# A selective state-space block with attention and feed-forward on one core: ScalarE's next exponential moved ahead of second halves of its jobs, and two kinds of VectorE reads moved one scan later

## The reference

```python
x = x + mamba(keep_top_rows(x))        # rows by norm; 512 channels, 16 states, L = 1024
# inside mamba, per batch:
xi, z  = split(rmsnorm(x) @ in_proj)
xi     = silu(causal_conv4(xi) + conv_b)
dt,B,C = split(xi @ x_proj)
delta  = softplus(dt @ dt_w + dt_b)
for t: h = exp(delta*A)*h + (delta*xi)*B ;  y = sum_s h*C     # 16 states s per channel
y      = (y + xi*D) * silu(z) ;  return x + y @ out_proj
x = x + feed_forward(attention(x, cond, mask))
```

## Time and profile before

| what | value |
|---|---|
| three executions | 580.72, 580.25, 576.88 us |
| median | 580.25 us |
| the profiled execution, its time | 581.45 us |
| its span in the profile | 579.3 us |
| granted TensorE clock, mean over the span | 0.926 |

### The profile page before, as it was taken

The page is one execution under the profiler, slowest core; times in us unless marked ns, Lnnn a source line. Parts: engine busy times, 40 slices in busy tenths (PEclk is TensorE's granted clock), DMA queues, the critical chain, the costliest instruction groups (busy, mean ns, idle before and its releaser), DMA issues.

```text
span 579.3 us, 7844 instructions
## 1 busy us (share of the span) xinstructions
PE 481.0 (83%) x2753; PEld 339.3 (59%) x2753; DVE 485.7 (84%) x569; ACT 352.5 (61%) x612; POOL 357.9 (62%) x215
## 2 busy tenths in 40 slices
PE   8968998789668999796689998966897867889992
PEld 6424664465457666554566665545785555878651
DVE  4779989987999899989998999799999989861512
ACT  3765666678765667886757768877466557521210
POOL 5039699747884698777856987787567548100001
PEclk9979999857999999979999999799998879699997
DMA  9331011110111011111110110111111860019004
GB/s 292 101 112 36 37 37 37 39 38 36 37 36 37 36 39 40 36 37 37 38 36 26 48 40 37 37 37 36 38 37 37 294 259 1 1 47 369 13 1 150
DMA packets 17918, 38.87 MB, mean 67 GB/s; under 512 B 1665, under 2 KB 10497, under 8 KB 17874
## 3 DMA queue, kind: packets, MB, share of 16 engines
q1 hardware_dynamic: 17874, 38.32, 19.0%
HBM read 36.08 MB, written 2.23 MB: 66 GB/s over the span
## 4 chain that ended last, share of the span: by engine, by line
PE 36%; DVE 33%; issue 16%; ACT 7%; POOL 6%; DVEq 0%; POOLq 0%; ACTq 0%
DVE scanmem L1686 19%; DVE yTd L1702 8%; PE hT L794 6%; PE pp L508 5%; POOL scanmem L1353 5%; PE pp L532 4%; PE pp L592 3%; PE yacc L566 3%; PE dA L765 2%; PE pp L558 2%; ACT hc L1227 2%; DVE yTd L1611 1%; PE pp L736 1%; PE yacc L562 1%; PE pp L664 1%
## 5 line engine op out<-in xcount | busy, mean ns | idle before, releaser
L1353 POOL TENSOR_TENSOR scanmem<-par,scanmem 128x1024 f32<-128x1024 f32 x128 | 299.1, 2362 | 94.7 <-PE hT L794 59.8
L1217 ACT ACTIVATE dA<-par,Aneg 128x512 f32<-128x512 f32 x256 | 172.5, 690 | 71.3 <-DVE scanmem L1686 70.2
L794 PE MATMUL hT<-con,scanmem 128*128 128x128 f32 x1024 | 158.7, 293 | 60.5 <-DVE yTd L1702 36.8
L794 PEld LDWEIGHTS hT<-con,scanmem 128*128 128x128 f32 x1024 | 122.0, 149 | 118.7 <-DVE yTd L1702 49.0
L1686 DVE TENSOR_TENSOR_SCAN scanmem<-dA,carry,scanmem 128x512 f32<-128x512 f32 x128 | 156.9, 1269 | 2.5 <-ACT dA L1217 2.4
L1686 DVE TENSOR_TENSOR_SCAN scanmem<-dA,scanmem 128x512 f32<-128x512 f32 x128 | 149.2, 1208 | 3.4 <-ACT dA L1217 3.0
L1227 ACT ACTIVATE hc<-hT,CTs 128x512 f32<-128x512 f32 x128 | 87.2, 681 | 78.1 <-PE hT L794 77.6
L1702 DVE SCALAR_TENSOR_TENSOR yTd<-hT,CTs,yTd 128x512 f32<-128x512 f32 x120 | 87.9, 733 | 10.9 <-PE hT L794 10.7
L566 PE MATMUL yacc<-con,hc 128*128 128x128 f32 x512 | 77.1, 293 | 5.8 <-ACT hc L1227 5.8
L566 PEld LDWEIGHTS yacc<-con,hc 128*128 128x128 f32 x512 | 63.2, 151 | 10.0 <-ACT hc L1227 6.5
L508 PE MATMUL pp<-xnT,wi 128*128 128x512 f32 x120 | 63.1, 658 | 5.1 <-ACT xnT L993 3.2
(11 more groups left out here) (194 smaller groups left out, 487.8 us busy)
## 6 DMA issues: line engine op xcount, KB each, us to landing
scanmem<-brow SPq DMA_DIRECT2D x32, 512.0 KB, 3.6
par<-in SPq DMA_DIRECT2D x1, 4096.0 KB, 18.1
scanmem<-in SPq DMA_DIRECT2D x1, 4096.0 KB, 15.1
xt<-in SPq DMA_DIRECT2D x4, 512.0 KB, 6.5
wi<-in SPq DMA_DIRECT2D x2, 1024.0 KB, 6.7
out<-par SPq DMA_DIRECT2D x4, 512.0 KB, 4.1
aw<-in SPq DMA_DIRECT2D x5, 256.0 KB, 6.6
xr<-in SPq DMA_DIRECT2D x1, 1024.0 KB, 8.8
```

Of the source, the lines that this page charges most:

```text
L794: last = nc.tensor.transpose(hT[:, i % 2, m * P:(m + 1) * P], hb[:, n % RING, m, i * P:(i + 1) * P], ident)
L1217: A(dA[:, m % 2, :], delta(c)[:, m, :], ACT.Exp, scale=Aneg[:, m * NS + s:m * NS + s + 1]).then_inc(da_ready, 1)
L1353: nc.gpsimd.tensor_tensor(hb[:, n % RING, ms, :], dx(c)[:, ms, :], Bb[:, row:row + 1, :].to_broadcast([P, 2, T]), ALU.mult).then_inc(bx_re ...
```

## The change

1. The tables. The first I job is tile 1 and the second tile 0, so POOL's tile comes one half earlier; POOL works its taps at states 5, 6 and 7 (before 4 and 5), its tanh is at half 12 (before 11) and its finish at state 9 (before 7). X goes from half 14 to 15, O 1 (chunks 1 and 2) from 16 to 17, D 2 from 20 to 21, D 3 from 21 to 22, the four Z from 22 to 25 to 23 to 26. POOL's dx products go from states 13 and 14 to 14 and 15.
2. ScalarE. Exponential 0 of state n + 1 is issued in state n, behind mul 2 and the first parts of the jobs of half 2n + 1, ahead of their second parts (V: Tanh; D: table load, Exp, Ln) and of the carry copy. In the even halves exponential 2 is issued between the first and the second parts.
3. VectorE. V and D jobs are read one half later, between scan 0 and scan 1 or between scan 2 and scan 3. All other jobs are read where they were.

```diff
--- before.py
+++ after.py
@@ -50,21 +50,23 @@
 
-PROLOGUE = {3: [("T", 0), ("T", 1)], 4: [("I", 0)], 5: [("I", 1)], 6: [("I", 2)], 7: [("I", 3)], 8: [("V", 0)],
-            10: [("V", 2)], 12: [("V", 3)], 14: [("X", 0)], 18: [("XT", 0), ("D", 0)], 20: [("D", 1), ("D", 2)], 21: [("D", 3)],
-            22: [("Z", 0)], 23: [("Z", 1)], 24: [("Z", 2)], 25: [("Z", 3)]}
-EPILOGUE = {1: [("Y", 1), ("Y", 3)], 11: [("O", 0)], 16: [("O", 1)], 28: [("R", 0)], 30: [("R", 1)]}
+PROLOGUE = {3: [("T", 0), ("T", 1)], 4: [("I", 1)], 5: [("I", 0)], 6: [("I", 2)], 7: [("I", 3)], 8: [("V", 0)],
+            10: [("V", 2)], 12: [("V", 3)], 15: [("X", 0)], 18: [("XT", 0), ("D", 0)], 20: [("D", 1)], 21: [("D", 2)], 22: [("D", 3)],
+            23: [("Z", 0)], 24: [("Z", 1)], 25: [("Z", 2)], 26: [("Z", 3)]}
+EPILOGUE = {1: [("Y", 1), ("Y", 3)], 11: [("O", 0)], 17: [("O", 1)], 28: [("R", 0)], 30: [("R", 1)]}
 LAST_EPILOGUE = {1: [("Y", 1)], 2: [("Y", 3)], 3: [("O", 0)], 5: [("O", 1)], 17: [("R", 0)], 19: [("R", 1)]}
 ATT = [6, 8, 8, 10, 12, 14, 15, 16, 17, 20, 22, 23, 24, 27]
 ATT1 = [28, 29]
 HEAD_CONV = 2
 EARLY_I = [2, 3, 0, 1]
 POOL_TILE = 1
-POOL_AT = [4, 5]
+FIRST_I = POOL_TILE
+POOL_AT = {5: range(0, 2), 6: range(2, 3), 7: range(3, KC)}
 SCALING_AT = 3
-DX_AT = [13, 14]
-POOL_TANH_AT = 11
-POOL_FINISH_AT = 7
+DX_AT = [14, 15]
+POOL_TANH_AT = 12
+POOL_FINISH_AT = 9
+LATE = ("V", "D")
 
 
 def product_convs(n):
@@ -144,6 +146,16 @@
 def to_read(h):
 
     return BESIDE[h - 1] if h else []
+
+
+def read_by_vector(h):
+
+    return [job for job in to_read(h) if job[0] not in LATE]
+
+
+def read_late(h):
+
+    return [job for job in to_read(h - 1) if job[0] in LATE] if h else []
 
@@ -994,7 +1006,7 @@
 
             def ev_I(job, o):
                 _, n, m = job
-                if m == 0:
+                if m == FIRST_I:
 
                     if n:
 
@@ -1022,8 +1034,11 @@
                     act.wait_ge(half_ready, 1)
 
                 A(xi(n)[:, m, :], o, ACT.Identity, bias=half_b[:, m:m + 1], scale=0.5)
+                return None
+
+            def product_tanh(job, o):
+                m = job[2]
                 A(o, o, ACT.Tanh, bias=half_b[:, m:m + 1], scale=0.5).then_inc(product_tanh_ready, 1)
-                return None
 
 
             def ev_X(job, o):
@@ -1142,8 +1157,8 @@
                     exp_ln_table()
                 if name == "D":
                     softplus(n, i)
-                if name == "S1":
-                    softmax(n)
+                if name == "V":
+                    product_tanh(job, bank(job))
 
             def read(job):
                 if job[0] in evs:
@@ -1151,7 +1166,8 @@
                     last = evs[job[0]](job, bank(job))
                     if last is not None:
                         last.then_inc(freed(job), 1)
-                after_job(job)
+                if job[0] == "S1":
+                    softmax(job[1])
 
             exp_ln_table()
 
@@ -1191,8 +1207,10 @@
             rstd(1)
             act.preload_act_table_set("exp_and_others")
             read(("V", 0, 2))
+            after_job(("V", 0, 2))
             conv_tanh(0, 0)
             read(("V", 0, 3))
+            after_job(("V", 0, 3))
             conv_tanh(0, 1)
             exp_ln_table()
             read(("X", 0, 0))
@@ -1235,21 +1253,29 @@
             for c in range(NCH):
                 for s in range(NS):
                     n = c * NS + s
-                    exp_step(n, 0)
+                    if n == 0:
+                        exp_step(n, 0)
                     exp_step(n, 1)
                     if n:
                         mul_step(n - 1, 0)
                     for job in to_read(2 * n):
                         read(job)
+                    exp_step(n, 2)
+                    for job in to_read(2 * n):
+                        after_job(job)
                     if c + 1 < NCH and 2 * s == POOL_TANH_AT:
                         pool_conv_tanh(c + 1)
-                    exp_step(n, 2)
                     exp_step(n, 3)
                     if n:
                         mul_step(n - 1, 2)
-                        carry_step(n - 1)
                     for job in to_read(2 * n + 1):
                         read(job)
+                    if n + 1 < NCH * NS:
+                        exp_step(n + 1, 0)
+                    for job in to_read(2 * n + 1):
+                        after_job(job)
+                    if n:
+                        carry_step(n - 1)
                     if c + 1 < NCH and 2 * s + 1 == POOL_TANH_AT:
                         pool_conv_tanh(c + 1)
             n = NCH * NS
@@ -1414,7 +1440,7 @@
                     if c + 1 < NCH and s in DX_AT:
                         step_times_input(c + 1, (0, 1) if s == DX_AT[0] else (2, 3))
                     if c + 1 < NCH and s in POOL_AT:
-                        conv_taps(c + 1, range(0, 2) if s == POOL_AT[0] else range(2, KC))
+                        conv_taps(c + 1, POOL_AT[s])
 
             pool.wait_ge(hT_ready, NCH * NS * NT)
             nc.gpsimd.memset(ff, 0.0).then_inc(ff_zero, 1)
@@ -1705,18 +1731,22 @@
                 for s in range(NS):
                     n = c * NS + s
                     scan_step(n, 0)
+                    for job in read_late(2 * n):
+                        read(job)
                     scan_step(n, 1)
                     if n:
                         mac_step(n - 1, 1)
-                    for job in to_read(2 * n):
+                    for job in read_by_vector(2 * n):
                         read(job)
                     scan_step(n, 2)
+                    for job in read_late(2 * n + 1):
+                        read(job)
                     scan_step(n, 3)
                     if n:
                         mac_step(n - 1, 3)
                     if s == 0 and c:
                         gate_even(c - 1)
-                    for job in to_read(2 * n + 1):
+                    for job in read_by_vector(2 * n + 1):
                         read(job)
                     if c == 0:
                         batch1_rows(s)
```

## The result

Six executions of the changed kernel have a median of 585.16 us (584.36 to 589.62), six of the kernel before on the same chip 580.38 us. The ratio is 1.0099 with a 95% interval of 1.0056 to 1.0143: slower by about 1%, 4.8 us. Times in this document are medians over all executions, while the ratios leave out executions in a slower state that the chip shows now and then whatever the kernel, so the two can differ by a few tenths of a per cent. The profiled execution took 585.59 us with a span of 583.5, where the one before had 581.45 and 579.3. So the profile's 4.2 us of span are nearly all of the difference, and can be looked for row by row.

What follows compares the result with a forecast made beforehand. VectorE was taken to limit the recurrence, its idle time being all that could be won. Won 5.7 us, lost 6.6, net 0.9 slower: 582.35 against the profiled execution, forecast 581; range 571 to 590, the forecast's own 576 to 586.

Steps and rivals of the forecast that it cites:

- D reads, at full clock: VectorE's D reads in the loop: of 10.5 us idle, 8.5 won by exponential 0 going first and later reads.
- Z reads: Z 0's read: some 0.4 us of its gap lost in two of three blocks, 0.9 won with rounding as stated.
- clock in the D stage: PE's granted clock at 0.50 beside D and Z jobs: 10.2 us in three blocks, half taken, 5.1 lost.
- V reads: V reads in the prologues of chunks 0 to 2: wait renamed from tanh to exponential, 1.0 us won by exceptions.
- softmax: Chunk 3: scan 2's 0.41 us wait behind S1's softmax goes, as exponential 2 now goes first; 0.4 won.
- O 1 in an odd half: Chunks 1 and 2: the transposes behind O 1 come late, so mac 1 waits 0.8 us each; 1.6 lost.
- X in an odd half, with POOL: X late: 1.7 us in chunks 1 and 2, 0.4 in chunk 0; POOL's late tile 1.2 in chunk 2.
- the sign: What would show the V chain: VectorE's idle time ahead of scans up by 2 to 3 us.
- The chain I worked out: At V: mul 2, Identity, exponential 0, scan 0, read, scan 1; scan 1 ends at 323.2 as before, nothing won.
- rival (c): Odd-half PE jobs delay transposes, clock low at Z 0: D stage -0.8, X, O 1, POOL 8; 588 us, chance 0.22.
- Rival (b): PE's clock holds through D jobs, odd halves cost half: 6.9 us won, 573.5 us; chance 0.20.

Runs made afterwards that it cites:

- v_early: Against d_spread: V read as in the kernel before, D still read late; 572.73 us, 0.9892 of the kernel before.
- o1_back: Against the changed kernel: O 1 put back from half 17 to 16; 580.15 us, 0.9999 of the kernel before.
- o_odd: Against d_spread: O 1 moved to half 17; 579.75 us, 1.0040 of the kernel before.
- x_odd: Against d_spread: X moved to half 15, with POOL's tile early; 579.84 us, 1.0031 of the kernel before.
- x_odd_warm: Against x_odd: 12 unused products added on PE in half 14 of chunks 0 to 2; 582.21 us, 1.0061 of the kernel before.
- d_spread: Against the changed kernel: X, O 1 and POOL back where they were before, D and Z jobs still one per half; 572.5 us, 0.9888 of the kernel before.
- tables_only: Against the kernel before: all tables of the change, with the old ScalarE and VectorE orders; 595.19 us, 1.0246.
- o1_back_finish8: Against the changed kernel: O 1 back in half 16 and POOL's finish at state 8 instead of 9; 580.52 us, 1.0038 of the kernel before.

## Why the prediction came out as it did

I forecast 581 us, within 1%, in a range of 571 to 590. The measured 585.2 lies in the range and just inside the forecast's own 576 to 586, at the upper edge of what I called within 1%. The losses were too small. The forecast called the change one that a measurement could not tell from none, and it was told. That it came out slower as forecast is partly luck, for I gave 0.27 to faster by over 1% and 0.24 to slower, and the number is near partly by luck too: a term for the clock that did not come (5.1 us) stood against losses at X and O 1 that I had too small by about 7 us.

| step | predicted | the profile after |
|---|---|---|
| D reads, at full clock | 8.5 won | 7.1 won (10.5 to 3.4 in the loop); 8.9 without the 1.9 that O 1 adds |
| Z reads | 0.9 won | 0.2 won |
| clock in the D stage | 5.1 lost | 0.5 lost |
| V reads | 1.0 won; the wait is renamed | renamed, 1.2 less in the rows; nothing in the time of `v_early` |
| softmax | 0.4 won | 0 |
| O 1 in an odd half | 1.6 lost | 5.5 of waits; 5.0 in `o1_back`, 7.2 in `o_odd` |
| X in an odd half, with POOL | 5.0 lost | 8.1 of waits; 7.3 in `x_odd` |

The sum of the scans' waits grew by 6.1 us, where I had named 2 to 3 as the sign: the rest stands behind X's copy and beside D 0.

**V.** The chain I worked out is what happens: 0.69 us ahead of the scan where 0.83 had stood ahead of the read. In chunk 0 the wait of 0.83 is gone and none stands in its place, as forecast. Over the loop 4.0 us ahead of V reads became 2.8 ahead of scans; that 1.2 us cannot be told in the time.

**D reads.** The size was right, but as a property of the edit it was wrong. I costed it as a sum of waits that go. The runs show that it needs both halves of the edit and a table with one D job per half: 0.2%, not clear of nothing, on the old table, 0.9% on the spread one.

**O 1.** This is the term that was mis-sized, and one step of it was left out. I priced only the mac step behind O 1: 0.8 a chunk, measured 0.80 and 1.04. I wrote that a job waits for the reader of the job two earlier when I described the kernel, and did not apply it here: D 0 is that later job. O 1's read moved one half later, D 0's products waited 1.25 us for it, and then the table load, Exp and Ln in a row. D 0's read shows 1.40 and 1.46 where I had 0.45; scans and a mac step beside it add 0.69 in chunk 1, 0.81 and 0.30 in chunk 2.

**X.** In chunk 1 the odd half cost 0.84 + 0.68 = 1.5 where I had 1.7, in chunk 2 with POOL 3.3 where I had 2.9, and PE waited 1.33 us for POOL's tile, forecast 1.2. In chunk 0 I had 0.4, for the ranking instruction covers it; it cost 2.57 + 0.68 = 3.3. The step that failed was the clock: I looked for it only at the D jobs, and not at the half that X leaves empty. PE's pause ahead of X was also longer in chunk 0 (3.18 us against 1.29 in chunk 1), where VectorE has the ranking instruction that I had taken for cover; no run leaves that instruction out, so its part in this is not shown. With the half filled, in `x_odd_warm`, chunk 0 costs only the scan's 0.67, near my 0.4. The Trainium skill, TensorE: Matmul & The Clock Gate, section HAM oscillation, has pauses between bursts bring the array back to half rate; I had cited it for rival (c) and worked out nothing at X. The windows above agree with this direction: 0.50 at X behind the emptied half, 1.00 with it filled. By that rule the spread D jobs would be at risk too, yet `d_spread` is the fastest of all.

**Softmax.** A reading mistake in the diff: the softmax moved from `after_job` into `read`, so it still stands ahead of exponential 2. The order did not change, nor did the wait.

**Clock in the D stage.** I took half of 10.2 us, as mac steps and scans that PE makes late. In states 10 to 12, beside D 1 to Z 3, they wait 0.5 us over the three chunks in the profile before and 1.0 after, besides the 0.99 counted at O 1. So this term was far too large here. Stretches at 0.50 still lie around the D and Z jobs, in other places in each profile, and the same sum is 0 in `d_spread` and 4.1 in `tables_only`; what decides it stays open. Rival (b) was right that the D stage would keep its gain, but it needed the odd halves to cost half of my figure, and they cost more. Rival (c) named the right mechanism for X and O 1; its D stage without gain did not come.

## What to carry to other kernels

When a job moves by half a step, follow its buffer as well as its engine: the next job in the same bank, and that job's slowest reader, may pay more than the one that stands behind it. Reordering a producer and delaying its reader are one edit: each alone only hands the wait to a neighbour, so test both, neither and each. And price an edit with the schedule that it will run under; the same reordering was worth 0.9 or 1.5% by where the jobs stood, and nothing that shows on the old table.

## What the runs showed of the hardware that I had not expected

- The clock at X in chunk 0 followed the half that X had left. In `x_odd` the granted clock fell from 1.00 to 0.50 (1.2 GHz) within the 4 us from 100 to 104, of which PE was busy 1.36 (their mean is 0.72), and X's eight products took 5.20 us; in `x_odd_warm`, with twelve products of no use in that half, it stayed at 1.00 and they took 3.63. In chunks 1 and 2, with the same half empty but PE's pause shorter, it did not fall.
- Stretches at the low clock are not tied to the program alone: X in chunk 0 fell into one in `o1_back_finish8` (mac wait 2.55 us) and less in `o1_back` (1.31), where chunk 0's program on PE is the same, and the mac wait of 1.90 us in chunk 3 comes and goes between kernels that run the same program there.
- A stall of 1.3 us that is seen to go, and 2.7 us won in the middle of the span, need not show in the time of a kernel whose executions spread over 4 to 10 us.
